# Three head groups instead of four, and folded values 512 columns wide, in the second attention of a fused two-layer transformer

## The reference

```python
x = x + L0_xattn(layernorm(x), ctx)            # 16 heads of 16, biases
x = x + L0_ffn(layernorm(x))                   # 4-bit weights, activations rounded to 16 bits
x = x + L1_xattn(layernorm(x), ctx, mask)      # the second attention, below
x = x + L1_ffn(layernorm(x))                   # 8 experts, softmax gate, best 2, weighted sum

# L1_xattn: 16 heads of 64, 77 context rows and one learned null row
q, k, v = heads(layernorm(x) @ Wq), heads(ctx @ Wk), heads(ctx @ Wv)
attn = softmax(where(mask, q @ concat(null_k, k).T, -max))
out  = layernorm((attn @ concat(null_v, v)) @ Wout)
```

## Time and profile before

| | us |
|---|---|
| median of 3 runs | 1119.86 |
| lowest, highest | 1117.01, 1123.49 |
| the profiled execution, own time | 1123.39 |
| its span on the core | 1121.7 |
| PE busy in the span | 1050.5 |
| DVE busy | 940.9 |
| ACT busy | 696.8 |
| POOL busy | 480.2 |

### The profile page before, as it was taken

One profiled execution on the slowest core, in us unless ns is written; L12 is line 12 of the kernel. 1 busy time (PEld: TensorE's weight loads), 2 busy tenths in 40 slices (PEclk: granted clock), 3 DMA queues, 4 the chain that ended last, 5 costly groups with the idle time before them and its releaser, 6 DMA issues.

```text
span 1121.7 us, 21070 instructions
## 1 busy us (share of the span) xinstructions
PE 1050.5 (94%) x6538; PEld 893.8 (80%) x6538; DVE 940.9 (84%) x2544; ACT 696.8 (62%) x1839; POOL 480.2 (43%) x543
## 2 busy tenths in 40 slices
PE   8999999998799888887798999999999899999997
PEld 6877788887688666443698999999999878788876
DVE  6799998886677699899566799999998788888885
ACT  2576777774355789578776677777776523333333
POOL 2335445442000477676001256666665443433343
PEclk9999999998699999689699999999999999999999
DMA  9000000000224387699301410111100000000000
GB/s 280 16 2 1 1 1 1 1 2 1 87 113 180 138 271 269 207 351 354 114 1 53 123 50 2 48 48 48 48 2 1 1 1 29 19 19 19 19 19 29
DMA packets 50647, 83.31 MB, mean 74 GB/s; under 512 B 4715, under 2 KB 36287, under 8 KB 50559
## 3 DMA queue, kind: packets, MB, share of 16 engines
q1 hardware_dynamic: 49183, 81.43, 21.3%
q10 hardware_dynamic: 1376, 0.79, 0.4%
HBM read 45.98 MB, written 36.23 MB: 73 GB/s over the span
## 4 chain that ended last, share of the span: by engine, by line
PE 42%; DVE 6%; issue 1%; POOL 1%; ACT 1%; DMA 1%; DVEq 0%; POOLq 0%; ACTq 0%
PE m_ps L2482 12%; PE a_ps L1282 10%; PE a_ps L1352 9%; PE f_ps L2383 5%; PE a_ps L1301 3%; PE m_ps L2506 1%; DMA k_raw<-vw_scratch 1%; PE a_ps L1331 1%; PE m_ps L2530 1%; DVE m_xl L2691 1%; DVE a_sm L1484 0%; DVE a_PTl L1508 0%; DVE a_mx L1500 0%; PE m_ps L2518 0%; DVE m_g L2678 0%
## 5 line engine op out<-in xcount | busy, mean ns | idle before, releaser
L1373 ACT ACTIVATE a_U<-a_ps,a_mx 128x80 f32<-128x80 f32 x512 | 125.7, 331 | 27.2 <-DVE a_mx L1500 24.4
L1443 POOL TENSOR_TENSOR a_xrs<-a_xve,mhalf 128x1 f32<-128x1 f32 x32 | 31.0, 969 | 156.6 <-DVE a_xve L1572 156.6
L2598 POOL TENSOR_TENSOR m_half<-m_half 128x512 f32<-128x512 f32 x32 | 41.0, 1281 | 118.1 <-ACT m_half L2558 118.1
L1450 POOL TENSOR_TENSOR a_U<-a_U,a_rc 128x1280 f32<-128x1280 f32 x32 | 74.6, 2333 | 35.9 <-DVE a_rc L1490 35.9
L2565 ACT ACTIVATE m_ex<-m_ls 128x8 f32<-128x8 f32 x32 | 6.7, 209 | 131.0 <-DVE m_ls L2654 131.0
L2482 PE MATMUL m_ps<-m_wh,m_xh 128*128 128x512 f32 x256 | 86.1, 417 | 0.0
L2230 POOL TENSOR_SCALAR f_sg<-f_sg 128x1024 f32<-128x1024 f32 x24 | 37.4, 1559 | 104.2 <-ACT f_sg L2119 103.8
L969 PEld LDWEIGHTS a_ps<-vals,a_PT 128*128 128x128 f32 x640 | 79.5, 198 | 2.2 <-issue 0.4
L2482 PE MATMUL m_ps<-m_wh,m_xl 128*128 128x512 f32 x256 | 80.5, 395 | 0.0
L2482 PE MATMUL m_ps<-m_wl,m_xh 128*128 128x512 f32 x256 | 80.2, 394 | 0.0
L1083 DVE TENSOR_SCALAR a_U<-a_ps 128x320 f32<-128x320 f32 x128 | 59.3, 484 | 24.6 <-PE a_ps L876 15.7
(11 more groups left out here) (270 smaller groups left out, 3343.4 us busy)
## 6 DMA issues: line engine op xcount, KB each, us to landing
up_scratch<-f_ub SPq DMA_DIRECT2D x24, 512.0 KB, 3.0
f_ul<-up_scratch SPq DMA_DIRECT2D x24, 512.0 KB, 5.7
key_scratch<-p_keys SPq DMA_DIRECT2D x8, 640.0 KB, 6.8
vw_scratch<-p_vw SPq DMA_DIRECT2D x16, 320.0 KB, 5.8
k_raw<-key_scratch SPq DMA_DIRECT2D x8, 640.0 KB, 5.3
k_raw<-vw_scratch SPq DMA_DIRECT2D x4, 1280.0 KB, 6.0
h_scratch<-f_hh SPq DMA_DIRECT2D x8, 512.0 KB, 2.7
h_scratch<-f_hl SPq DMA_DIRECT2D x8, 512.0 KB, 3.2
```

The source lines that it names most:

```text
L1373: last = act.activation(U[a.p][:, h * KP:(h + 1) * KP], bank(a, g)[:, (h % 4) * KP:(h % 4 + 1) * KP], ACT.Exp, bias=mx[a.p][:, h:h + 1])
L1450: pool.tensor_tensor(heads(U[a.p]), heads(U[a.p]), rc[a.p][:].unsqueeze(2).broadcast_to([P, H, KP]), ALU.mult).then_inc(s_N, 1)
```

## The change

Scores: the groups are now 6, 6 and 4 heads, that is 480, 480 and 320 columns, each with a bank of its own (`S[g]`); 18 products per tile instead of 24. A group's bank waits for the exponentials of the same group of the tile before. DVE's maxima follow: `top(0)` and `top(1)` read 480 columns, `top(2)` reads 320, `top(3)` is gone.

Values: high and low folded values lie side by side in one tile, and one product of 512 columns multiplies the high numerators with both, into the two halves of `Y`; the low numerators are multiplied with the high values into the first half. 20 products (10 of 512 columns, 10 of 256) instead of 30 of 256. The halves are added outside: ACT copies the second half to `yb` (now at the head of its step), and DVE adds the first half to it behind `top(1)`. PE's next values product waits for that addition (`s_y3`).

```diff
 # tensor
             def scores(a, g):
-                if 4 * a.t0 + g >= 3:
-                    pe.wait_ge(s_E, 4 * a.t0 + g - 2)
+                if a.t0 >= 1:
+                    pe.wait_ge(s_E, a.of(lambda n: NG * (n - 1) + g + 1))
...
                     if t.t0 >= 1:
-                        pe.wait_ge(s_y2, t.of(lambda n: n))
+                        pe.wait_ge(s_y3, t.of(lambda n: n))
+                    v = fold.values[t.batch % 2]
+                    for k, js in enumerate(PTS):
+                        pe.wait_ge(s_PTe, t.of(lambda n: 3 * n + k + 1))
+                        for j in js:
+                            pe.matmul(Y[:].rearrange("p (i d) -> p i d", i=2), PTs[t.p][:, j, :], v[:, :, j, :],
+                                      start=(j == 0), stop=False, skip_group_check=True)
+                    for k, js in enumerate(PTS):
+                        pe.wait_ge(s_PTl, t.of(lambda n: 3 * n + k + 1))
+                        for j in js:
+                            last = pe.matmul(Y[:, 0:D], PTl[t.p][:, j, :], v[:, 0, j, :],
+                                             start=False, stop=(j == NJ - 1), skip_group_check=True)
                     last.then_inc(s_y, 1)
 # scalar, first in body(t); the old copy behind exps(a, 0) is gone
+                if c_.ok():
+                    act.wait_ge(s_y, c_.of(lambda n: n + 1))
+                    if c_.t0 >= 2:
+                        act.wait_ge(s_x1, c_.of(lambda n: n - 1))
+                    act.copy(yb[c_.p][:], Y[:, D:2 * D]).then_inc(s_y2, 1)
 # vector, body(t)
                 top(1)
                 if t.ok() and t.t0 >= 2:
                     dve.wait_ge(s_y, t.of(lambda n: n - 1))
+                prev = t + -1
+                if prev.ok():
+                    dve.wait_ge(s_y2, prev.of(lambda n: n + 1))
+                    dve.tensor_tensor(yb[prev.p][:], Y[:, 0:D], yb[prev.p][:], ALU.add).then_inc(s_y3, 1)
                 probs(0)
                 top(2)
...
-                top(3)
```

```diff
+            act.activation(mx[1][:, 0:1], c["nneg"][:, 0:1], ACT.Exp)
             for t in range(FIRST, LAST + 1):
                 body(At(t))
-                if t == FIRST + 1:
+                if t == FIRST + 2:
                     for q in range(4):
                         value_high(0, q)
```

```diff
+        if self.ends_early(m, half):
+            pe.wait_ge(self.s_km, self.NM)
+        elif m == self.NM - 1:
+            pe.wait_ge(self.s_We, 4 * m)
+        elif 2 * m + half >= 1:
             pe.wait_ge(self.s_We, 2 * (2 * m + half))
```

More of the change, by code:

```diff
@@ L290, in _ @@
             steps(m, 1)
-            steps(a, 1)
-            steps(m, 1)
-            steps(a, 1)
+            steps(a, 2)
             steps(m, 1)
@@ L520, in __init__ @@
         high1, low1 = self.place("k_high1", [P, KT, SW], F32R), self.place("k_low1", [P, KT, SW], F32R)
-        vhigh1, vlow1 = self.place("VW_high1", [P, NJ, D], F32R), self.place("VW_low1", [P, NJ, D], F32R)
+        values1 = self.place("VW1", [P, 2, NJ, D], F32R)
         self.high, self.low = [high0, high1], [low0, low1]
-        self.vhigh, self.vlow = [vhigh0, vhigh1], [vlow0, vlow1]
+        self.values = [values0, values1]
+        self.vhigh, self.vlow = [[v[:, i, :, :] for v in self.values] for i in range(2)]
         self.raw_values = self.raw[:].rearrange("p k n -> p (k n)").rearrange("p (j d) -> p j d", d=D)
@@ L724, in folded_key, with ends_early, value_banks, staging @@
                   self.k1[m % 2][hh * D1:(hh + 1) * D1, :], start=True, stop=True).then_inc(self.s_A, 1)
+    def ends_early(self, m, half):
+        return m == self.NM - 1 and half == 0
+    def value_banks(self, m, half):
+        return (self.KB, self.VB) if self.ends_early(m, half) else self.WB
+    def staging(self, m, half):
+        if m == self.NM - 1 and half == 1:
+            return self.keys[0][0:KP].rearrange("p k b n -> p (k b n)")[:, 0:4 * D].rearrange("p (h n) -> p h n", h=2)
+        return self.stage[half][:]
     def folded_value(self, pe, m, half):
@@ L1213, in attention1, with columns, width @@
     FIRST, LAST = -5, NT + 1
+    GROUPS = [range(0, 6), range(6, 12), range(12, H)]
+    NG = len(GROUPS)
+    def columns(g):
+        return slice(GROUPS[g][0] * KP, (GROUPS[g][-1] + 1) * KP)
+    def width(g):
+        return len(GROUPS[g]) * KP
     with ExitStack() as st:
@@ L1409, in body @@
                 if a.ok():
-                    for g in range(1, 4):
+                    for g in range(1, NG):
                         exps(a, g)
@@ L1814, in ffn @@
         T, R, Y = ps[0:2], ps[2:6], ps[4:8]
[L1815 removed]
+        top = [ps[6], ps[7], ps[6], None, ps[2]]
         (sh, sga, sup, ssl, kup, ksl, ih, kga, spr, kpr, tmp, sps) = [sc[:, i:i + 1] for i in range(12)]
```

75 lines of the change are left out of this document (29 added, 46 removed).

## The result

After takes 1146.71 us, the median of 4 runs (1143.09 to 1149.74); before, on the same chip, 1119.18 (4 runs, 1117.01 to 1123.49). The ratio is 1.0226, 95% interval 1.0198 to 1.0253: slower by 2.3%. The forecast was 1144 (1130 to 1156). The profiled execution of after took 1143.09, with a span of 1141.4 us and a mean granted clock of 0.963.

What follows compares the result with a forecast made beforehand. The prediction took PE to bound the kernel before the change. Terms +30.2 - 6.0 - 2.7 + 3.0 - 0.1 = +24.4 on the profiled 1123.39 gave 1147.8, or 1144 us on the median; range 1130 to 1156.

Steps and rivals of the forecast that it cites:

- The bound: Attention steps 1 to 23: PE has no idle time, so its list sets the step of 8.41 us.
- PE's own work: Each attention step on PE: fewer, wider scores and values products save 0.12 us together.
- The loop through DVE: Attention steps: PE's values product waits for DVE's addition, so a step goes from 8.41 to 9.57 us; steps 1 to 28 +30.2.
- PE's idle time: Each attention step: PE stands idle 1.16 to 1.2 us waiting for DVE's addition.
- The other loop: Attention steps, through POOL's x1 and ACT's copy: 9.13 us long, so hidden behind 9.57 with 0.4 to spare.
- The first tile: Start of this attention: PE's 3.77 us wait for `xnT` and the low clock after it go; -6.0 us, bounds -8 to -1.
- The fold's end: Behind the fold's last maxima: the transposition `rows_max(4)` no longer waits behind two value products; -2.7 us, bounds -3 to 0.
- The end of the attention: Steps 29 to 32: values products wait for sums and additions on DVE; +3 us, bounds -1 to +8.
- rival 1: Attention steps: the addition is ready in time and PE stays the bound; -12.2 us, 1108; chance 0.06.
- The loop through POOL and ACT: Rival for the attention steps: DVE's loop is shorter than thought and this one binds at 9.13 us; 1131; chance 0.12.
- rival 3: Attention steps: the clock falls in PE's new gaps, every third step or each; 1164 to 1206 us; chance 0.07.

Runs made afterwards that it cites:

- e6: after with three buffers `yb` and the addition at the head of DVE's step, ahead of the first maxima; 1115.95 us, ratio to before 0.9944.
- e9: e2 with three buffers `yb` and ACT's copy of Y at the head of ACT's step; 1117.13 us, ratio to before 0.9950.
- e7: after with one more 320-column maxima reduction on DVE, result unused, directly ahead of the second maxima; 1158.44 us (one run).
- e4: after with DVE's addition moved ahead of the second maxima, still behind the sums; 1137.27 us (one run).
- e3: after with four 320-column groups in three rotating banks and ACT's copy back behind the first exponentials; 1125.90 us, ratio to before 1.0023.
- e5: after with three buffers `yb` instead of two, the addition still behind the second maxima; 1139.50 us (one run).
- e8: after with one more 320-column maxima reduction on DVE, result unused, behind the addition and ahead of the third maxima; 1148.96 us (one run).
- e10: e1 with after's order of the last steps, two attention steps together ahead of the experts' first tile; 1116.23 us (one run).
- e1: before with only the fold's last pair through more banks, and first values one step later with an early dummy exponential; 1114.67 us, ratio 0.9917.
- e2: e1 with only the three head groups (480, 480, 320 columns, fixed banks), values and release of Y as before; 1117.03 us, ratio 0.9957.

## Why the prediction was right, point by point

- **The bound.** PE without idle time in steps 1 to 23 became PE waiting for `a_yb` of L1546 in each step, as foreseen from the release of Y.
- **PE's own work.** Forecast -0.12 us a step. e6, where only PE's list counts, has 8.34 against 8.41: -0.07. The groups give 0.02 (e9) and the values 0.05. A 480-column product takes (725.69 - 724.81) / 4 = 0.220 and not 0.218, which over twelve of them is the 0.02 that is missing. The first pair behind transposes takes 0.53 instead of 0.44, but before has the same there (0.38 instead of 0.29). The two-part moving operand costs no more than one of 512 columns: in e6, where nothing waits, ten products take 2.33, 0.233 each, against 0.2317.
- **The loop through DVE.** Leg by leg, forecast and then measured: transposes 0.79, 0.79; first group until DVE takes it up 1.65, 1.67; first maxima 0.57, 0.57; sums to reciprocal 1.92, 1.92; second maxima 0.51, 0.51; addition 0.415, 0.41; hand-over 0.09, 0.05; values with the restart 3.62, 3.64. Sum 9.57 and 9.56. e7, e4 and e3 changed three of the legs by 0.40, 0.51 and 0.74, and the step followed by 0.41, 0.56 and 0.74.
- **PE's idle time**: forecast 1.16 to 1.2 a step. The rows show 0.93 on PE and 1.2 on its weight loads, which is the truer number, since the modelled ends of the products ahead cover the rest: after's step is 1.21 longer than e6's, in which PE does the same work and does not wait.
- **The other loop.** Forecast 9.13, with 0.4 to spare. `xnT` is done at 728.59 and `xnl` starts at 729.45, so 0.86 was to spare: the numerators took 1.22 in place of 1.44 and the six exponentials 1.27 in place of 1.47, as mean durations overlap in a row of small instructions. The mechanism was right, the length 0.4 too long. By e4, it was no bound even at 8.99.
- **The first tile.** Forecast -6.0, measured -5.3, and -2.8 to -5.8 in the experiments. The 3.77 us went and the low clock with it. PE has 2.1 us less idle time there, where 3.8 was forecast, and is busy for 3.2 less, where 2.2 was forecast, so two errors partly cancel. What is late next is not tile 0's exponentials; it is the last down products' sum on DVE, for which step 0 waits 2.29 where it waited 0.67 before. PE of after in order of time:

```profile
617.93 1.06 PE L1325 MATMUL a_ps<-ident,a_U 128*128 128x128 f32 x8 [2.29 <-DVE xs L2372]
```

- **The fold's end.** -2.7 and -2.7, with the transposition 0.15 us behind the maxima's end, where "within 0.3" was asked.
- **The end of the attention.** +3 and +2.95, but the agreement is partly luck. I had priced sums and additions at full clock. In after, step 29 takes 12.98 us against 10.59, and of these 2.39 only 0.95 is more idle time of PE; 1.44 is PE busy for longer, at a mean grant of 0.87 in place of 1.00. Its values product waited 2.39 us and then ran slowly (PE of after in order of time):

```profile
901.35 3.42 PE L1372 MATMUL a_ps<-VW,a_PT 128*128 128x512 f32 x10 [2.39 <-DVE a_yb L1546]
```

The stretch of that product, in the table of busy time of after, at a mean grant of 0.67:

```profile
901.35:906.50 5.15, 5.15 (x21) 4.48 (x21) 3.52 (x10) 1.96 (x9) 2.92 (x4) 0.67 0.00 0
```

  Step 30 is 0.78 shorter than before's, and what follows it 1.33 longer. Every kernel with the addition loses at the end: 1.0 us in e5, 2.0 to 2.5 in e3, e4, e6, e7 and e8. In e6, where steps 29 and 30 stay at a grant of 1.00, it is 2.4, so the clock is not all of it. The order costs 0.2 (e10). How the loss divides in after stays open.

- **The rivals.** The addition was not in time (rival 1; e6, where it is, shows what that looks like). The loop through POOL and ACT did not bind (e4, e5). The clock stayed at 1.00 through all of steps 1 to 28, with a gap in every step, so rival 3 did not come true in the steady part, though the grant fell in step 29, as above. The rule on depth-cycling in the Trainium skill ("TensorE: Matmul & The Clock Gate", A second HAM failure mode: psum-queue depth-cycling) did not show with gaps of 1.2 us in 9.55.

The change loses by the place of one addition. Four versions beat before, by less than 1%: e1 with the outer parts alone, e2, e6 and e9. Their ratios, 0.9917, 0.9957, 0.9944 and 0.9950, have intervals that overlap, so none is shown to be the best. By the length of the steps e6's loop is the fastest, but at the end e6 takes 2.4 us more than e1, and it wins only 1.9 before (1.6 in steps 1 to 23, 0.3 in the next five).

## What to carry to other kernels

- When an edit moves the release of a buffer to another engine, write down the round from the waiting engine's step start to its next: the instructions ahead of the new releaser on its engine, back to what *they* wait for. If that is something the waiting engine makes in the same step, the sum of the legs is the new step, however idle both engines look. Put the releaser ahead of the first such wait.
- Wider groups save little on the engine that computes them (0.02 us a step here) and lengthen each round that passes through a first group, by product, maxima and exponentials together.
- The largest wait of a profile may be worth nothing (75 us on ACT), and a small one the whole loss. To tell them apart, put the same work inside and outside the supposed round.

## What was not expected of the hardware

- After single waits the granted clock fell in some executions and not in others of nearly the same length. PE waited for the down products' sum ahead of step 0 in most kernels. After waits of 2.81, 2.81, 2.78 and 2.73 us (e4, e5, e7, e8) step 0 ran at a mean grant of 0.83 to 0.85 and took 9.87 to 9.95 us; after 2.71 (e2), 2.29 (after) and 2.10 (e6) it ran at 1.00 and took 8.37 to 8.41. Step 0 of e8 in the table of busy time:

```profile
622.89:632.84 9.95, 9.95 (x50) 8.80 (x51) 5.88 (x12) 6.04 (x21) 2.33 (x1) 0.83 1.05 313
```

Step 0 of e2:

```profile
626.39:634.80 8.41, 8.41 (x60) 7.98 (x61) 5.85 (x12) 5.93 (x21) 2.33 (x1) 1.00 1.07 308
```

  So the wait that is late next behind the 3.77 us can lose 1.5 us again in some executions. Whether that is part of the 3.6 us by which after's median lies above its profiled execution stays open.
- The low-clock stretch at the end of the first attention varies between executions of kernels that are alike there. It is missing in after and e5 alone. They take 25.1 us from the start of the last products with the keys to the feed-forward part, and the other ten kernels 31.7 to 32.2, though before and after have the same two waits ahead of it, of 0.76 and 1.49 us. The executions also come to it up to 6.3 us apart, with mean grants between 0.64 and 1.00 in their first 30 us, which I did not follow further. Together this shifts all that follows by up to 10 us, more than all parts of this change outside the loop together.
